# First value weighting of a unit at the end of its sub-step, in a ring of five exponent buffers

## What is computed

```python
x = x + tanh(g_xattn[0]) * L0_xattn(layernorm(x), ctx, ctx)      # 16 heads, softmax over 1500 keys
x = x + tanh(g_ffn[0])   * L0_ffn(layernorm(x))                  # 8 experts of 512, best 2 by softmax
x = x + tanh(g_xattn[1]) * L1_xattn(layernorm(x), ctx, ctx, mask)
x = x + tanh(g_ffn[1])   * L1_ffn(layernorm(x))                  # 8 experts of 64, sigmoid gates, plus a shared one
```

## Time and profile before

| what | us |
|---|---|
| median of three runs | 967.49 |
| the three runs | 967.49, 957.93, 972.21 |
| the profiled execution, its own time | 965.04 |
| its span, first to last instruction | 963.2 |

### The profile page before, as it was taken

One profiled execution on the slowest core, in us unless ns is written; L12 is line 12 of the kernel. 1 busy time (PEld: TensorE's weight loads), 2 busy tenths in 40 slices (PEclk: granted clock), 3 DMA queues, 4 the chain that ended last, 5 costly groups with the idle time before them and its releaser, 6 DMA issues.

```text
span 963.2 us, 33056 instructions
## 1 busy us (share of the span) xinstructions
PE 861.1 (89%) x13273; PEld 620.4 (64%) x13273; DVE 697.7 (72%) x1545; ACT 591.7 (61%) x1085; POOL 538.8 (56%) x733
## 2 busy tenths in 40 slices
PE   3898899898899988989999999998999999999975
PEld 1365667676666766767667666666766666666754
DVE  4778777858778686776757858787777868687724
ACT  2267576565755757666575576757676666757570
POOL 5647754546456364654556557676675667672202
PEclk9989999999999999999999999999999999999995
DMA  5344543212222222223667747687776766675300
GB/s 149 96 131 127 164 120 98 90 47 77 79 81 88 62 66 71 87 76 94 125 113 148 145 86 149 136 170 141 154 146 134 160 123 152 122 143 108 59 2 19
DMA packets 103555, 104.48 MB, mean 108 GB/s; under 512 B 28442, under 2 KB 97388, under 8 KB 103404
## 3 DMA queue, kind: packets, MB, share of 16 engines
q1 hardware_dynamic: 101792, 102.03, 45.6%
q10 hardware_dynamic: 1612, 0.36, 0.2%
HBM read 35.89 MB, written 0.46 MB: 38 GB/s over the span
## 4 chain that ended last, share of the span: by engine, by line
PE 56%; DVE 20%; ACT 11%; issue 6%; POOL 3%; ACTq 1%; DMA 1%; SPq 0%; POOLq 0%; DVEq 0%
PE pO L1295 12%; PE pST L1274 11%; DVE mx L1153 10%; PE pMX L1316 9%; PE pKV L1361 5%; PE pKV L1352 5%; ACT P L856 3%; PE pF L1425 3%; PE pF L1461 3%; ACT HR L865 2%; ACT L856 2%; DVE HR L1033 1%; ACT V L888 1%; DVE rden L1078 1%; ACT L865 1%
## 5 line engine op out<-in xcount | busy, mean ns | idle before, releaser
L1153 DVE TENSOR_REDUCE mx<-pMX 112x1 f32<-112x500 f32 x768 | 490.3, 668 | 101.7 <-PE pMX L1316 97.3
L856 ACT ACTIVATE P<-pST 125x448 f32<-125x448 f32 x768 | 389.5, 542 | 226.6 <-PE pST L1274 222.7
L1316 PE MATMUL pMX<-kop,qmax 48*112 48x500 f16 (+1 forms) x768 | 277.2, 403 | 12.0 <-DMA qmax<-qlo 6.9
L1274 PE MATMUL pST<-qexp,kop 50*128 50x112 f16 (+2 forms) x3072 | 268.2, 215 | 19.8 <-ACT P L856 16.6
L1274 PEld LDWEIGHTS pST<-qexp,kop 50*128 50x128 f16 (+2 forms) x3072 | 182.8, 100 | 99.1 <-ACT P L856 42.6
L1295 PE MATMUL pO<-P,V 125*18 125x112 f32 x6144 | 189.4, 265 | 4.5 <-issue 4.4
L1295 PEld LDWEIGHTS pO<-P,V 125*18 125x18 f32 x6144 | 139.2, 99 | 39.1 <-issue 19.8
L665 POOL CAST khi<-kfull 128x500 f16<-128x500 f32 x96 | 57.6, 600 | 140.9 <-ACT kfull L883 140.5
L1316 PEld LDWEIGHTS pMX<-kop,qmax 48*112 48x112 f16 (+1 forms) x768 | 97.7, 131 | 57.2 <-DVE mx L1153 20.1
L667 POOL TENSOR_TENSOR klo<-kfull,khi 128x500 f16<-128x500 f32 x96 | 109.1, 1136 | 7.8
L794 POOL TENSOR_TENSOR Clo<-C,Chi 128x500 f16<-128x500 f32 x93 | 105.7, 1136 | 7.5
(11 more groups left out here) (170 smaller groups left out, 1195.9 us busy)
## 6 DMA issues: line engine op xcount, KB each, us to landing
C<-in_ctxT SPq DMA_DIRECT2D x31, 750.0 KB, 7.4
kop<-maskop SPq DMA_DIRECT2D x48, 437.5 KB
kop<-khi SPq DMA_DIRECT2D x192, 62.5 KB
kop<-khi SPq DMA_DIRECT2D x96, 125.0 KB
kop<-klo SPq DMA_DIRECT2D x96, 62.5 KB
kop<-klo SPq DMA_DIRECT2D x48, 125.0 KB
maskin<-in_mask SPq DMA_DIRECT2D x8, 656.2 KB, 4.9
qexp<-qmax SPq DMA_DIRECT2D x16, 182.0 KB
```

The lines of the kernel that those rows point to most:

```text
L856: nc.scalar.activation(P[0:KP, slot, h * 4 * T:(h + 1) * 4 * T], pST[0:KP, h, 0:4 * T], ACT.Exp, scale=EXP_SCALE).then_inc(exp_done, 1)
L1153: nc.vector.tensor_reduce(mx[:, s % 2, c, p:p + 1], pMX[0:T, m % 3, 0:CW], AX.X, ALU.max).then_inc(max_done, 1)
L1274: mm = nc.tensor.matmul(pST[0:keys.stop - keys.start, h, i * T:(i + 1) * T], kop[rows, b, slot, keys], qexp[rows, b, slot, :, :].rearrange ...
L1316: nc.tensor.matmul(pMX[0:T, m % 3, 0:CW], qmax[rows, b, slot, :, :].rearrange("r j q -> r (j q)"), kop[rows, b, slot, c * CW:(c + 1) * CW] ...
```

## The change

`weigh` of sub-step 6 (`AV_LAG + 1`), the first pair of each unit, moves behind `project` in steps of layer 0, and behind score half 1 in steps of layer 1, in both cases still ahead of the small products at the end of the sub-step. The ring gets a fifth slot, and its slots run on across units, since 12 is no multiple of 5. To make room, the 261 columns of broadcast constants (`bc`) share the buffer of the expert products (`ysc`), which is first written later; the one number of them that is still read then, `route_scale`, is copied to a tile of its own in step 1.

```diff
-RING = 4
+RING = 5
...
-        bc = sb("bc", [128, NBC])
+        route = sb("route", [128, 1])
...
-        ysc = sb("ysc", [T, 2, 4, D])
+        products = sb("products", [128, 2 * 4 * D])
+        ysc = products[0:T, :].rearrange("t (k e d) -> t k e d", k=2, e=4)
+        bc = products[:, 0:NBC]
...
-                slot = tile % RING
+                slot = (KT * (st.s - back) + tile) % RING
...
-                dve.wait_ge(init_l, 8)
+                nc.vector.tensor_copy(route[:, :], bc[:, RS:RS + 1]).then_inc(init_l, 1)
+                dve.wait_ge(init_l, 9)
...
-                            link(nc.vector.tensor_scalar(gp[:, :], g2[:, :], bc[0:T, RS:RS + 1], None, ALU.mult))
+                            link(nc.vector.tensor_scalar(gp[:, :], g2[:, :], route[0:T, :], None, ALU.mult))
...
                             score_half(st, kt, h)
                             if h == 0:
                                 mids(kt)
-                        weigh(st, kt)
+                        if kt != AV_LAG + 1:
+                            weigh(st, kt)
                         project(kt)
+                        if kt == AV_LAG + 1:
+                            weigh(st, kt)
                     else:
                         if apart_ and not late:
                             max_scores(st, m0)
-                        weigh(st, kt)
+                        if kt != AV_LAG + 1:
+                            weigh(st, kt)
                         score_half(st, kt, 0)
...
                         score_half(st, kt, 1)
+                        if kt == AV_LAG + 1:
+                            weigh(st, kt)
```

More of the change, by code:

```diff
@@ L1295, in weigh @@
                             mm = nc.tensor.matmul(pO[32 * g:32 * g + VW, r * T:(r + 1) * T],
-                                                  V[0:KP, b, tile, p, :], P[0:KP, tile % RING, p * T:(p + 1) * T],
+                                                  V[0:KP, b, tile, p, :], P[0:KP, (KT * (st.s - back) + tile) % RING, p * T:(p + 1) * T],
                                                   start=(tile == 0 and r == 0), stop=(tile == KT - 1),
@@ L1324, in step @@
                 if s == 3:
-                    pe.wait_ge(init_l, 8)
+                    pe.wait_ge(init_l, 9)
                     pe.wait_ge(f_in, 16 * 4)
```

## The result

The changed kernel takes 974.16 us (median of 20 runs, 968.68 to 981.61); the kernel before, in 20 runs, 966.54 (957.93 to 972.21). The ratio is 1.0084, with a 95% interval of 1.0064 to 1.0105: slower by 0.8%, some 7.6 us, where 0.8 us less was forecast. The time lies inside the range of 954 to 975, near its upper end. The profiled execution of after has a span of 970.9 us, 7.7 more than that of before, so the two traces show a difference of the measured size; with a spread of 13 us among the 20 runs that is in part luck.

A forecast was written before the change was run, and what follows sets the result against it. PE was taken to set the pace (56% of the chain), DVE at some places (20%). Terms 0 + 0 + 0 - 0.3 - 0.5 + 0 = -0.8 us, set on a mean of 965.7, gave 964.9 us; range 954 to 975.

The forecast's parts named there:

- Even steps of layer 1: Eight steps, 16 to 30: "sum" takes over the weighting's wait, "gT" starts as before; zero, bounds 7.1 us lost, 7.0 won.
- Even steps of layer 0: Six steps with a "gT", 4 to 14: weighting and k2 change places, "gT" still goes at rden; zero.
- Odd steps: Sixteen steps: PE issues the same pieces without a gap in another order; zero, 1.6 us either way.
- The clock rival: Clock falls in sub-step 6, even steps of layer 1, at 1.2 us each: 9.6 us, 974.5; chance 0.13.
- The two ends: Step 2's score half 0 waits less for ACT, 0.3 us won; step 32's "gT" less for rden, 0.5 won.
- Waits that really go: Layer 1's waits at the weighting (4.1 us) and "gT" (1.6) vanish, 6.5 us with the ends: 959.2; chance 0.15.
- the ring as a hidden limit: With a fifth slot exponents run ahead and PE's waits for ACT go: below 946 us possible; chance 0.03.

The follow-up runs named there:

- l1only: Changed kernel with layer 0 back in the old order: ring of five kept, weighting moved in layer 1 alone; 964.69 us, ratio 0.9992 to the kernel before.
- ringonly: Changed kernel with all weightings back in the old order, leaving only the ring of five and the shared buffer; 967.24 us, ratio 1.0001 to the kernel before.
- samelength: Changed kernel without the query projection's bias product in steps 1 to 13, two idle products in its place; 963.59 us, ratio 0.9964 to the kernel before.
- shorter: Kernel before without the bias product of the query projection in steps 1 to 13 of layer 0; 967.10 us, ratio 1.0001.
- fillbefore: Kernel before plus idle products in PE's waits: ahead of h0, xT and "ct" in layer 0, y0 in even steps of both layers; 961.41 us, ratio 0.9964.
- lag: Kernel before with two idle products of 240 columns behind k2 in the odd steps of layer 0; 980.71 us, ratio 1.0138.
- covered: Kernel before with two idle products of 240 columns ahead of "gT" in even steps of layer 0, in the wait for rden; 966.43 us, ratio 1.0000.

## Why the prediction was wrong

The step that failed is the one from moved pieces to the sum: the prediction added up the work and the waits that move, with the odd steps at zero, and gave the clock no term, since it looked for falls only at the waits that change. The runs showed 0.20 us more in each odd step of layer 0, and by that length some four to six more falls of the clock there, at 1.5 us each. The prediction also held that some 2%, 19 us, could not be told from no change; 20 runs tell 0.8%.

**Even steps of layer 1: right.** The wait moved from the weighting to "sum" (0.47 us in step 22) and to "gT" (0.38, forecast about 0.5), 3.83 us from the first maximum to "gT" stayed, the first maximum to "q" in odd step 21 stayed at 2.45, and l1only shows nothing won or lost.

**Even steps of layer 0: right.** 28.76 us with and without the change, where the clock holds.

**Odd steps: the term that failed.** The prediction put them at "zero, with 0.1 us per step either way for another sequence of 16-bit and 32-bit products". In layer 1 it is 0.03. In layer 0 it is 0.20, twice the bound: the weighting behind k2 and "q" behind the weighting each brought 0.1. The sum had the doubt at the right place, with too small a bound and another reason: the weighting and "q" are both products in 32 bits, so the new order changes between 16 and 32 bits less often than the old one (once from score half to "q", where it was three times). What the rows show is the weight load that no longer starts ahead of its product, at two places. By itself that is 1.6 us, and would have left the forecast right.

**The clock rival: right mechanism, wrong place.** The clock was given 0.13, and at 1.2 us a fall, at most 1.7; measured 1.5. But it was to decide "in each step whose sub-step 6 shows a granted clock under 1.00", in the even steps of layer 1. Sub-step 6 kept its clock. The falls came in layer 0, sub-steps later (those at 292.4 and 302.6 some 9 and 19 us behind the moved weighting), at waits that the change left as they were. I looked for new waits; the experiments show that a length is enough. That its time, 974.5, was the measured one is luck: its sum is another.

The Trainium skill, "TensorE: Matmul & The Clock Gate", section "HAM oscillation — how this bites in real kernels", has the clock fall after one long gap between products. The rows don't bear that out: in the two windows of after that precede a fall PE's longest waits were 0.64 and 0.59 us, in 3.40 us of which it was busy for 2.17 and 2.13. They are nearer to the section "A second HAM failure mode: psum-queue depth-cycling", by which many short pauses are enough, though the same pauses were followed by no fall in before (284.0 to 287.4).

**The two ends: right for step 32** (-0.57 against -0.5; the traces of all seven kernels with the new order in layer 1 have it). In step 2 the score half waited 0.28 us in place of 0.45, 0.17 less against the 0.3 taken, within its bounds; the longer wait at that step's end is not the change's.

**Waits that really go, and the ring as a hidden limit:** neither; waits in layer 1 are 5.7 us before and after, and ringonly is at 1.0001.

**The size.** Over all runs the mean clock of after is 0.964 and that of before 0.971 to 0.973. 0.007 of some 970 us, each fall half of 3.4 us, is (0.007 x 970) / 1.7 = 4 more falls an execution, at 1.5 us some 6 us, and with 0.009 it is 5 and some 7.7 us; with 1.6 for the odd steps and 0.7 won in steps 2 and 32 that is an estimate of 6.9 to 8.6, against 7.6 measured. It takes the clock of the start and the end as the same in both on average.

**What stays open.** Why 0.2 us more per odd step brings the falls, why 0.2 less (samelength) brings none, and why 0.4 less (shorter) didn't give its 2.8 us back. The steps repeat with a fixed length, and the same waits (2.17 us busy in 3.40) are followed by a fall in one step and not in another; how the repeating pattern meets the clock's control is a guess that no run here tests. The falls of after are not spread evenly over layer 0: four stand in successive steps (292.4, 302.6, 353.8 and 364.1 us), one alone 109 us before them and one 109 us behind them. Why the weight loads no longer run ahead in the new order is open too.

## What to carry to other kernels

Where PE is busy for most of the time and its clock falls now and then, a sum of moved waits is not enough: compare the granted clock by stretch in both profiles, and its mean over all runs, before any step is blamed for a difference. A small growth of a step that repeats (0.2 us in 29) can cost several times its size by that way, and idle products in the waits ahead of the falls, as many as the wait covers, both show the cause and win time: fillbefore, at 0.9964, has the lowest median of this study. When products change places, look at whether the weight load of each still starts ahead of it; the two that lost this cost about 0.1 us each here.

## What was unexpected of the hardware

- Two windows of 3.40 us with the same 2.17 us of PE time and the same two waits, at the same place of the program: a fall to 1.2 GHz behind one (after), none behind the other (before).
- 1.6 us of idle products in PE's path cost some 13 us (lag), and the same products in PE's waits cost nothing (covered); twenty-one in each pair of steps of layer 0 and four in each of layer 1, in the waits, won 3.5 us by the ratio of 0.9964 (fillbefore).
- The first product of "q", 128x112 in 32 bits, took 0.41 us of PE's pace behind the weighting and 0.31 behind k2; k2 took 0.74 ahead of the weighting and 0.64 ahead of "q". The shorter times go with a weight load that starts 0.20 us ahead of its product.
